# Loading x by image and channel at the start of a fused convolution chain, and its rows later

## The chip, the cores and the metric

The kernel runs on one core of a Trainium2 chip. A core has TensorE (PE in the profile), VectorE (DVE), ScalarE (ACT) and GpSimd (POOL), each with an instruction queue of its own, and SyncE (SP), which here only issues transfers. Sixteen DMA engines move all data between device memory and the on-chip buffer; SP, ACT and POOL can each put transfers on them. The metric is device microseconds (us) of one execution; less is better.

## The reference

The input x has 8 images, 16 channels and 64 x 64 pixels. Four blocks follow each other, each of the form `x = x + f(norm(x))`:

```
x = x + _L0_conv_ref(_gn(x), L0_conv_W, L0_conv_b)
x = x + _L1_conv_ref(_gn(x), L1_conv_weight)
x = x + _L2_conv_ref(_gn(x), ...)
x = x + _L3_conv_ref(_gn(x), L3_conv_combinator, L3_conv_bias)
```

`_gn` takes mean and variance of each image over groups of two channels and all pixels. The first block is a lattice of 4 x 4 cells; each cell is a 3 x 3 convolution with bias and ReLU that reads one to three results of other cells (16 channels each) and gives up to three. Only the last result, added to x, leaves the lattice. The other three blocks are single convolutions (one circular, one over spline features of the pixels, one plain).

## The kernel before, in words

**Layouts.** In the lattice a pixel row y of the image is cut as y = 4 q + r: the four rows r lie in different partitions, and even and odd pixel columns (s) in different halves, so a tile of one image has 2 x 4 x 16 = 128 partitions (s, r, channel) and 16 x 32 = 512 pixels. `X` holds all 8 images in this layout. Inputs and outputs of the cells lie in device memory (`lattice`, called `LAT` in the code), 32 rows of 2180 numbers for an image, where a row stands for a channel and a parity of the pixel row and is padded with zeros.

**Start, in the order of the text.** Each engine has its own stream of instructions; semaphores order them. SP and POOL load x into `XROW` by 32 transfers of 16 x 16 x 64 numbers, that is runs of one pixel row of 64 numbers, 256 bytes (L720, L812). ACT issues the small loads (identity `IDF`, raw weights `RAW`, biases, constants `CB` and `G`); TensorE waits for all six constants (`const_loaded`) before its first instruction. DVE clears buffers (`WX`, `KS`, the gaps, pieces of the weights, and the staging buffer `ST`, 128 x 6543 numbers). TensorE turns the weights of cell 0 (L1624), ACT and DVE split them into a high and a low part (L1077, L1274), POOL stores them as taps in device memory (`store_taps`, L845), clears the buffer (L838) and loads them spread over the partitions into `WA` (`spread_cell`, L853). DVE and ACT copy x from `XROW` to `X` (L1289, L1134), DVE takes statistics of each image (L1298, L1302), TensorE averages over the partitions of a group (L1693), DVE and POOL make scale and shift (POOL: L820, L822). ACT normalises one image at a time into one of three slots of `KS` (L1081), and POOL stores each by 4 transfers into `lattice` (L948), 32 in all.

**The lattice.** The 16 cells run one after the other, 8 images each: 128 steps (k, b), cell and image. For each step SP loads the input from `lattice` into one of four raw slots (L761), ACT rounds it to the high part (`split_hi`, L1098), DVE makes the low part and copies (`split_lo`, L1398 to L1410), TensorE multiplies (L1662), ACT adds the bias and applies ReLU into `ST` (`evacuate`, L1109), SP stores the result (L744), four steps behind the loads. ACT and DVE split two pieces ahead of TensorE. POOL spreads the weights of the next cell while one runs and waits at the end of each step for its evacuation. At cell 15 DVE adds the result to `X`; the later blocks work from there.

Of the kernel before, what the change touches and what calls it, by code (L numbers as in the profile page):

```python
# [6 lines left out]
P = 128  # L7
C = 16
WD = 64
# [10 lines left out]
YB = 8  # L20
BASES = 8
# [129 lines left out]
def build(nc, x, l0w, l0b, l1w, l2base, l2spline, l2scale, l2bias, l3w, l3bias, consts, out):  # L151
# [58 lines left out]
    RAW_STEPS.update({(8, 6): 12, (9, 4): 13, (10, 0): 14, (10, 6): 15})  # L210
    TURNS = ["cell0", "cell1"] + [TURN_STEPS[step] for step in sorted(TURN_STEPS)]
# [18 lines left out]
    with ctx:  # L230
# [47 lines left out]
        XROW = flat[:, 0:HALF * RQ * WD].rearrange("p (i y w) -> p i y w", i=HALF, w=WD)  # L278
        XS = KS[:, 0:3 * TOP].rearrange("p (z f) -> p z f", z=3)
# [57 lines left out]
        x_loaded = [sem(f"x_loaded{i}") for i in range(HALF)]  # L337
        x_loaded_pool = [sem(f"x_loaded_pool{i}") for i in range(HALF)]
        x_split, x_split_act = sem("x_split"), sem("x_split_act")
        const_loaded = sem("const_loaded")  # L340
# [9 lines left out]
        st_clear = sem("st_clear")  # L350
# [9 lines left out]
        input_stored = [sem(f"input_stored{b}") for b in range(B)]  # L360
        image_loaded = [sem(f"image_loaded{q}") for q in range(SLOTS_K)]
        tp_stored = sem("tp_stored")
        w_loaded = [sem("w_loaded0"), sem("w_loaded1")]
        w1_loaded, w2_loaded, w3_loaded = sem("w1_loaded"), sem("w2_loaded"), sem("w3_loaded")
# [6 lines left out]
        xn_ready = sem("xn_ready")  # L371
# [56 lines left out]

        def staged(s):

            return ST[:, s % SLOTS_S]

        def target_row(p, b, o, r):

            m = 1 if p is None else cells[p].m
            return first_row[p] + b * m * HALO + (r * m + o if m < 3 else 2 * o + r) * C
# [41 lines left out]
        def output_stores(s):  # L478
# [11 lines left out]
            else:  # L490
                yield from image_store(k, b, st)

# [169 lines left out]
        for par in range(2):  # L662
            n = 0
            for cell in cells[par::2]:
                n += dma_total(cell_spread(cell))
                w_after[cell.k] = n
# [48 lines left out]
        def _(sp):  # L715
            xv = x.rearrange("b c (q r) w -> b r c q w", r=4)
# [13 lines left out]
            load_taps(2)  # L730

# [14 lines left out]
            for s in range(STEPS):  # L746
# [9 lines left out]
                if k == 0:  # L756
                    sp.wait_ge(input_stored[b], 4 * 16)
                else:
                    sp.wait_ge(image_stored[b], 16 * stores_before[k])
# [46 lines left out]
        def _(pool):  # L806

            xv = x.rearrange("b c (q r) w -> b r c q w", r=4)
            for b in range(B):
                for y in range(2, 4):  # L810
                    rows = b % 2 * 4 * C + y * C
                    pool.dma_start(XROW[rows:rows + C, b // 2], xv[b, y]).then_inc(x_loaded_pool[b // 2], 16)  # L812
# [131 lines left out]
            norm(slice(0, B), slice(0, B), 1)  # L944
            for b in range(B):
                pool.wait_ge(xn_ready, b + 1)
                for dst, src in image_store(None, b, XS[:, b % 3]):
                    pool.dma_start(dst, src).then_inc(input_stored[b], 16)  # L948
            for s in range(STEPS):
# [6 lines left out]
                if k == 5 and b == 0:  # L956
                    for image in range(B):
                        pool.wait_ge(input_stored[image], 4 * 16)
# [14 lines left out]
                if k in (1, 2) and b in (1, 3):  # L973
                    half = 2 * (k - 1) + b // 2
                    pool.memset(flat[4 * C:P, half * PIECE:(half + 1) * PIECE], 0.0).then_inc(kr_clear, 1)
                if k + 1 < NC and k != 12:
# [85 lines left out]
        def _(act):  # L1062
            act.dma_start(IDF[:, :], consts[0:NG * C, P:P + NG * C]).then_inc(const_loaded, 16)
            for k in range(2):
                act.dma_start(RAW[k][:, :], l0w[0, k].rearrange("o i k d -> o (i k d)")).then_inc(raw_loaded[k], 16)
            act.dma_start(BN_IN[:, :], l0b.rearrange("a r (g c) -> (a r g) c", c=C)).then_inc(const_loaded, 16)
            act.dma_start(CB[:, :], consts[:, P + NG * C:P + NG * C + CB_COLUMNS]).then_inc(const_loaded, 16)
            act.dma_start(G[:, :], consts[:, 0:P]).then_inc(const_loaded, 16)
            act.dma_start(OB_IN[0:1, :], l2bias.rearrange("(a c) -> a c", a=1)).then_inc(const_loaded, 16)
            act.dma_start(OB_IN[1:2, :], l3bias.rearrange("(a c) -> a c", a=1)).then_inc(const_loaded, 16)  # L1070
# [59 lines left out]
            for i in range(HALF):  # L1130
                act.wait_ge(x_loaded[i], 4 * 16)
                act.wait_ge(x_loaded_pool[i], 4 * 16)
                for s in range(2):
                    last = act.activation(X[s * 4 * C:(s + 1) * 4 * C, 2 * i + 1].rearrange("p (y w) -> p y w", w=RX),  # L1134
                                          XROW[4 * C:P, i].rearrange("p y (w s) -> p s y w", s=2)[:, s], ACT.Copy)
                last.then_inc(x_split_act, 1)
            turned_hi_part("cell1")
            act.wait_ge(st_clear, 1)
            for b in range(B):
                act.wait_ge(norm_ready, 1)  # L1140
                if b >= 3:
                    act.wait_ge(input_stored[b - 3], 4 * 16)
# [706 lines left out]
```

## Time and profile before

| | |
|---|---|
| median of 3 runs | 1314.58 us (1313.54 to 1317.95) |
| the profiled execution | 1317.47 us, of which its span is 1315.7 us |
| busy share of the span | PE 89%, PEld 66%, DVE 59%, ACT 51%, POOL 30% |
| first and last convolution matmul of the lattice | 59.68 us and 1050.7 us into the span |
| moved by DMA | 232.12 MB, mean 176 GB/s |

The span is what the profile shows of the execution; the rest lies around it. PE is TensorE's matmuls, PEld its loading of weights, which runs beside them. A queue's name with a small q (SPq, POOLq) means the issuing of transfers.

### The profile page before, as it was taken

What the parts mean: (1) busy time and instruction counts of PE and PEld (TensorE: products, weight loads), DVE (VectorE), ACT (ScalarE), POOL (GpSimd) and SP (SyncE); (2) the same over time, 40 slices, a digit from 0 to 9 for tenths busy, and PEclk for the clock granted to TensorE, in tenths of its full rate; (3) what the DMA queues carried; (4) which work ended last, traced back from release to release, by engine and by line L of the source; (5) the groups of instructions that cost most, each with busy time, mean ns of one, the idle gap of its engine ahead of it and who ended that gap; (6) DMA issues with size and microseconds to landing.
All of it is one profiled execution on the core that took longest, in us unless ns stands there. A gap on an engine that the chain in (4) does not pass through costs nothing.

```text
span 1315.7 us, 14861 instructions
## 1 busy us (share of the span) xinstructions
PE 1175.0 (89%) x5088; PEld 870.3 (66%) x5088; DVE 775.1 (59%) x962; ACT 671.9 (51%) x724; POOL 391.3 (30%) x570
## 2 busy tenths in 40 slices
PE   1278898979999999999999999999999856999995
PEld 1155566756666667776666677777777745777773
DVE  5478895246656452225565653225665679899962
ACT  2357774335454444443545444334434588789921
POOL 5724243234450102122114032632123432103212
PEclk9999999989999999999999999999999977999997
DMA  9489998899999977889999996977789314577783
GB/s 88 122 205 232 243 279 228 221 189 188 221 194 218 192 195 193 220 194 171 217 196 206 213 225 175 254 210 211 193 190 204 53 31 70 84 115 120 114 125 57
DMA packets 108751, 232.12 MB, mean 176 GB/s; under 512 B 41332, under 2 KB 55236, under 8 KB 100484
## 3 DMA queue, kind: packets, MB, share of 16 engines
q1 hardware_dynamic: 91552, 205.02, 70.0%
q0 software_dynamic: 16576, 25.89, 10.7%
q8 instruction: 40, 0.66, 0.2%
q10 hardware_dynamic: 548, 0.27, 0.2%
q14 instruction: 35, 0.29, 0.1%
HBM read 122.05 MB, written 85.75 MB: 158 GB/s over the span
## 4 chain that ended last, share of the span: by engine, by line
PE 54%; SPq 15%; DVE 12%; issue 6%; DMA 6%; ACT 4%; POOL 3%; ACTq 0%; DVEq 0%; POOLq 0%
PE PB L1662 46%; SPq L761 11%; PE PB L1633 6%; SPq L744 3%; DMA S<-lattice 2%; DVE S L1500 2%; DVE F L1398 2%; ACT F L1098 2%; DVE S L1494 2%; DVE F L1410 2%; DVE F L1487 1%; DVE S L1507 1%; DMA F<-F 1%; PE PB L1624 1%; DMA lattice<-S 1%
## 5 line engine op out<-in xcount | busy, mean ns | idle before, releaser
L1662 PE MATMUL PB<-F,WA 128*96 128x512 f32 (+1 forms) x3792 | 922.0, 404 | 54.8 <-DVE F L1410 31.2
L1662 PEld LDWEIGHTS PB<-F,WA 128*96 128x96 f32 (+1 forms) x3792 | 663.6, 176 | 303.9 <-issue 56.0
L1098 ACT ACTIVATE F<-S 128x2116 fp32r<-128x2116 f32 (+4 forms) x160 | 261.7, 1637 | 271.5 <-DMA lattice<-S 122.3
L1109 ACT ACTIVATE S<-PB,BIAS 96x512 f32<-96x512 f32 (+1 forms) x320 | 209.5, 681 | 235.2 <-PE PB L1662 234.9
L1398 DVE TENSOR_TENSOR F<-S,F 128x1089 fp32r<-128x1089 f32 (+2 forms) x80 | 121.4, 1518 | 197.6 <-ACT F L1098 197.1
L1410 DVE CAST F<-F 64x528 fp32r<-64x528 f32 (+4 forms) x304 | 190.3, 675 | 3.5
L1400 DVE TENSOR_TENSOR F<-S,F 128x1058 fp32r<-128x1058 f32 x64 | 80.7, 1261 | 185.7 <-ACT F L1098 185.0
L1633 PE MATMUL PB<-F,WA 128*128 128x512 f32 x576 | 148.5, 416 | 20.6 <-DVE F L1487 20.6
L853 POOL DMA_DIRECT2D WA<-taps x84 | 61.0, 729 | 350.7 <-ACT S L1109 335.8
L1633 PEld LDWEIGHTS PB<-F,WA 128*128 128x128 f32 x576 | 113.2, 198 | 50.2 <-issue 21.8
L1401 DVE TENSOR_TENSOR F<-S,F 64x1058 fp32r<-64x1058 f32 x64 | 82.0, 1281 | 0.0
L845 POOL DMA_DIRECT2D taps<-WX x112 | 69.5, 685 | 22.6 <-ACT S L1109 13.5
L820 POOL TENSOR_TENSOR RS<-VE,NHALF 128x1 f32<-128x1 f32 (+1 forms) x25 | 25.1, 1003 | 129.4 <-DVE VE L1323 129.3
L838 POOL MEMSET WX<- 48x1600 f32 x18 | 26.1, 1452 | 116.6 <-ACT S L1109 94.7
L1404 DVE TENSOR_TENSOR F<-S,F 128x1089 fp32r<-128x1089 f32 x16 | 20.7, 1296 | 43.7 <-ACT F L1098 43.7
L1208 ACT ACTIVATE F<-S 128x2112 fp32r<-128x2112 f32 x16 | 31.5, 1968 | 26.8 <-DVE S L1507 14.5
L1081 ACT ACTIVATE KAN<-X,NBI,RS 64x512 f32<-64x512 f32 (+1 forms) x48 | 32.6, 679 | 20.1 <-POOL NBI L822 11.1
L1184 ACT ACTIVATE S<-KS,CB 128x528 f32<-128x528 f32 x64 | 41.9, 726 | 0.3
L1633 PE MATMUL PB<-F,WX 128*128 128x512 f32 x96 | 29.9, 471 | 13.5 <-DMA F<-F 13.5
L1487 DVE SCALAR_TENSOR_TENSOR F<-S,F 128x1056 fp32r<-128x1056 f32 x32 | 39.0, 1260 | 3.1 <-ACT F L1208 3.1
L1042 POOL DMA_DIRECT2D out<-OT x26 | 14.7, 579 | 84.8 <-DVE OT L1475 84.8
L1494 DVE SCALAR_TENSOR_TENSOR S<-S 128x2112 f32<-128x2112 f32 x16 | 37.7, 2354 | 2.4 <-ACT S L1192 2.4
(122 smaller groups left out, 720.3 us busy)
## 6 DMA issues: line engine op xcount, KB each, us to landing
lattice<-S SPq DMA_DIRECT2D x48, 817.5 KB, 6.3
S<-lattice SPq DMA_DIRECT2D x448, 66.1 KB, 5.1
lattice<-S SPq DMA_DIRECT2D x96, 272.5 KB, 4.0
S<-lattice SPq DMA_DIRECT2D x160, 136.1 KB, 3.0
S<-lattice SPq DMA_DIRECT2D x72, 272.5 KB, 5.5
S<-lattice SPq DMA_DIRECT2D x160, 70.1 KB, 2.9
S<-lattice SPq DMA_DIRECT2D x80, 136.2 KB, 4.9
S<-lattice SPq DMA_DIRECT2D x160, 66.0 KB, 2.9
```

The source lines that it names most:

```text
L761: sp.dma_start(dst, src).then_inc(image_loaded[q], 16)
L845: pool.dma_start(dst, src).then_inc(tp_stored, 16)
L853: pool.dma_start(dst, src).then_inc(w_loaded[k % 2], 16)
L1098: act.activation(piece_view(s, h, 0), raw_view(s, h), ACT.Copy).then_inc(hi_ready, 1)
L1109: act.activation(wide(to[:, at:at + TS])[:, :, 0:RX], pixels(RING_BANK[n % SLOTS_O][0:cell.rows, :]), ACT.Relu, bias=BIAS[0:cell.rows, k:k ...
L1398: last = nc.vector.tensor_tensor(lo, raw, hi, ALU.subtract)
L1400: nc.vector.tensor_tensor(lo[:, 0:2], raw[:, 0:2], hi[:, 0:2], ALU.subtract)
L1401: last = nc.vector.tensor_tensor(lo[0:4 * C, 2:4], raw[0:4 * C, 2:4], hi[0:4 * C, 2:4], ALU.subtract)
L1410: last = nc.vector.tensor_copy(FP[4 * C:P, slot, part, to:to + n], FP[0:4 * C, slot, 0, source:source + n])
L1494: nc.vector.scalar_tensor_tensor(A2[n % 2], AA[n % 2], 2.0, A2[n % 2], ALU.subtract, ALU.mult)\
L1633: last = nc.tensor.matmul(pixels(bank[:, :]), weights, moving, start=open_ and n == 0, stop=close and n == len(todo) - 1)
L1662: last = nc.tensor.matmul(bank, WA[0:rows, first:first + cell.rows], wide(FZ[0:rows, i % SLOTS_F, base:base + TS])[:, :, 0:RX], start=j == ...
```

## The change

x is loaded in its own order: 128 partitions are (image, channel), 4096 pixels each, in four transfers of 128 x 1024 numbers on SP into the memory of `X`, seen as `XC`. DVE takes statistics of 8 pieces of 512 pixels as they arrive and joins them into one mean and variance for each partition; TensorE averages over a pair of channels with a matrix `PAIR_MEAN`, made from `G`. Scale and shift are now one number for each partition. ACT and DVE normalise half of x each, in four instructions of 128 x 512 (`XN_ORDER`), into `XN`, which has the layout of `lattice` with all images below each other; SP stores images 0 and 1 by two transfers of 32 rows (`input_stores(0)`), POOL images 2 to 7 by two transfers of 96 rows.

Around it: SP, not POOL, loads cell 0's weights into `WA`; POOL, not DVE, clears `ST`; the weight and bias work that cell 0's start does not need follows the normalisation on DVE; TensorE's first instruction waits for `IDF` and `RAW` alone. The rows of x in the lattice's layout, which cell 15 adds, are loaded in the lattice: `X_LOADS` names eight steps of cells 7, 8, 11, 12, 13 and 14 in which POOL loads one image through `OT` by four transfers of 16 x 16 x 64, and two steps later (`X_SPLITS`) DVE and ACT copy half of it each into `X`. The edge values of the spline block are made by DVE at step (8, 3).

```diff
+    X_LOADS = {(7, 2): 0, (8, 1): 1, (8, 5): 2, (11, 3): 3, (12, 3): 4, (13, 1): 5, (13, 5): 6, (14, 2): 7}
+    X_SPLITS = {(k, b + 2): image for (k, b), image in X_LOADS.items()}
...
+        def input_stores(i):
+            rows = slice(0, FIRST * C) if i == 0 else slice(FIRST * C, P)
+            for r in range(2):
+                yield LAT[r * P + rows.start:r * P + rows.stop], XN[rows, r * PIECE:(r + 1) * PIECE]
...
-            for b in range(B):
-                for y in range(2):
-                    rows = b % 2 * 4 * C + y * C
-                    sp.dma_start(XROW[rows:rows + C, b // 2], xv[b, y]).then_inc(x_loaded[b // 2], 16)
+            xc, n = x.rearrange("b c h w -> (b c) (h w)"), HT * WD // XPARTS
+            for i in range(XPARTS):
+                sp.dma_start(XC[:, i * n:(i + 1) * n], xc[:, i * n:(i + 1) * n]).then_inc(channel_loaded[i], 16)
...
+            sp.wait_ge(tp_stored, tp_after["cell0"])
+            for dst, src in cell_spread(cells[0]):
+                sp.dma_start(dst, src).then_inc(w0_loaded, 16)
+            sp.wait_ge(xn_act, 1)
+            sp.wait_ge(xn_dve, 1)
+            for dst, src in input_stores(0):
+                sp.dma_start(dst, src).then_inc(input_stored[0], 16)
...
+            pool.memset(ST[:, :, :], 0.0).then_inc(st_clear, 1)
+            def load_x(b):
+                xv = x.rearrange("b c (q r) w -> b r c q w", r=4)
+                if b >= 2:
+                    pool.wait_ge(x_split, b - 1)
+                    pool.wait_ge(x_split_act, b - 1)
+                for y in range(4):
+                    pool.dma_start(OT[y * C:(y + 1) * C, b % 2], xv[b, y]).then_inc(x_loaded[b % 2], 16)
...
+            norm(slice(1, 2), slice(0, 1), 1)
             clear_taps("cell1")
-            spread_cell(0, 0, 1)
+            pool.wait_ge(xn_act, 1)
+            pool.wait_ge(xn_dve, 1)
+            for dst, src in input_stores(1):
+                pool.dma_start(dst, src).then_inc(input_stored[1], 16)
             store_taps("cell1")
...
             turned_hi_part("cell0")
+            act.wait_ge(norm_ready, 1)
+            act.wait_ge(xn_clear, 1)
+            for r, s, h in XN_ORDER[0::2]:
+                last = normalise(xn_rows(r, s, h), channel_rows(r, s, h), 0)
+            last.then_inc(xn_act, 1)
             turned_hi_part("cell1")
...
+                if (k, b) in X_SPLITS:
+                    image = X_SPLITS[k, b]
+                    dve.wait_ge(x_loaded[image % 2], 4 * 16 * (image // 2 + 1))
+                    nc.vector.tensor_copy(pixels(X[0:4 * C, image]), row_halves(image, 0)).then_inc(x_split, 1)
...
-            pe.wait_ge(const_loaded, 6 * 16)
-            pe.wait_ge(wa_clear, 1)
+            pe.wait_ge(idf_loaded, 16)
```

SP's stream from its first transfer to the first image loaded from `lattice`, before; a row is a line, what it writes and reads, its shape, and the semaphores it waits for:

```order
L720 DMA S<-in_x 16x16x64 x16
L727 DMA RAW_ONE<-in_L_conv_weight 16x144
L728 DMA RAW_ONE<-in_L_conv_combinator 16x144
L724 DMA RAW<-in_L_conv_W 48x432 [waits turned]
L761 DMA S<-lattice 32x1089 [waits input_stored0]
L761 DMA S<-lattice 32x561
L761 DMA S<-lattice 32x528
```

The same stretch of SP's stream after:

```order
L747 DMA X<-in_x 128x1024 x4
L754 DMA RAW_ONE<-in_L_conv_weight 16x144
L755 DMA RAW_ONE<-in_L_conv_combinator 16x144
L751 DMA RAW<-in_L_conv_W 48x432 [waits turned]
L760 DMA WA<-taps 64x4x64 [waits tp_stored]
L760 DMA WA<-taps 64x4x64
L760 DMA WA<-taps 64x2x64 x2
L760 DMA WA<-taps 64x4x64 x2
L760 DMA WA<-taps 64x2x64 x2
L764 DMA lattice<-S 32x2180 [waits xn_dve,xn_act]
L764 DMA lattice<-S 32x2180
L795 DMA S<-lattice 32x1089 [waits input_stored0]
```

Sixteen short loads are gone, and the eight weight loads and two long stores stand ahead of the first image.

POOL's stream from its first transfer to the scale of the normalisation (`RS`), before:

```order
L812 DMA S<-in_x 16x16x64 x16
L813 MEMSET TWOS 128x1
L814 MEMSET NHALF 128x8
L845 DMA taps<-WX 16x4x128 x8
L838 MEMSET WX 48x1600
L853 DMA WA<-taps 64x4x64 x2
L853 DMA WA<-taps 64x2x64 x2
L853 DMA WA<-taps 64x4x64 x2
L853 DMA WA<-taps 64x2x64 x2
L845 DMA taps<-WX 144x1x32 x8
L820 ISA
L820 TENSOR_TENSOR RS<-VE,NHALF 128x8
```

The same stretch of POOL's stream after, to the second taps:

```order
L842 MEMSET TWOS 128x1
L843 MEMSET NHALF 128x8
L844 MEMSET S 128x6543
L884 DMA taps<-WX 16x4x128 x8
L859 ISA
L859 TENSOR_TENSOR RS<-VE,NHALF 128x1
L861 TENSOR_TENSOR NBI<-GM,RS 128x1
L877 MEMSET WX 48x1600
L985 DMA lattice<-S 96x2180 x2
L884 DMA taps<-WX 144x1x32 x8
```

The 16 loads of x and cell 0's weight loads are gone, the clearing of `ST` (here `S`) has come, and the taps of cell 1 now stand behind the two stores.

POOL's stream in cell 7 after, around the load of image 0 (step (7, 2)); before, the same rows stood there without the two of L854:

```order
L892 DMA WA<-taps 64x1x288 [waits evac_done,out_done,tp_stored]
L854 DMA OT<-in_x 16x16x64 [waits evac_done]
L854 DMA OT<-in_x 16x16x64 x3
L892 DMA WA<-taps 64x1x288 x2
L877 MEMSET WX 48x1600 [waits tp_stored,evac_done]
L892 DMA WA<-taps 64x1x288
```

Four loads of x now stand ahead of later weight loads of the next cell.

## Rows read from the trace of the kernel before

**Rows 1.** The chain of work that ended last, first 60 us: start, length, what.

```profile
4.92 8.79 DMA OB_IN<-in_L_conv_bias
...
21.51 7.21 DMA taps<-WX
...
39.35 1.73 POOL RS L820
...
42.56 9.37 POOL lattice L948 x19
...
55.73 1.11 ACT F L1098
...
59.68 5.47 PE PB L1662 x12
```

**Rows 2.** Busy time, clock and DMA share by stretch (us from start: length, engines).

```profile
0.00:59.70 59.70, 4.57 (x43) 3.94 (x43) 27.85 (x85) 16.75 (x22) 41.80 (x81) 1.00 0.76 113
...
495.00:541.00 46.00, 46.00 (x205) 36.58 (x204) 10.96 (x9) 19.29 (x25) 9.72 (x13) 1.00 0.77 204
...
858.00:894.00 36.00, 36.00 (x165) 28.52 (x164) 9.81 (x9) 14.09 (x17) 8.43 (x11) 1.00 0.74 203
```

**Rows 3.** Timeline of the start: start, length, engine, line, what [idle before].

```profile
0.74 13.93 SPq L720 DMA_DIRECT2D S<-in_x  x16
1.13 1.39 DVE L1261 MEMSET WX<- 48x1600 f32 x1 [1.13 <-PEq L1836]
...
7.45 5.51 DVE L1269 MEMSET S<- 128x6543 f32 x1 [1.43 <-issue]
...
13.75 1.15 PE L1624 MATMUL PB<-IDF,RAW 48*16 48x32 f32 x18 [13.75 <-DMA OB_IN<-in_L_conv_bias]
...
14.98 1.28 ACT L1077 ACT_TABLE_LOAD   x1 [14.98 <-PE PB L1624]
...
16.71 0.44 DVE L1274 TENSOR_TENSOR WX<-PB,WX 16x288 fp32r<-16x288 f32 x1 [1.67 <-ACT WX L1077]
...
17.79 4.23 POOL L845 DMA_DIRECT2D taps<-WX  x8 [7.28 <-DVE WX L1274]
...
31.30 4.82 DVE L1298 BATCH_NORM_STATS2 STATS<-X 128x6 f32<-128x512 f32 x8
...
36.15 0.64 DVE L1302 BATCH_NORM_AGGREGATE MV<-STATS 128x2 f32<-128x6 f32 x8
...
41.45 2.23 ACT L1081 ACTIVATE KS<-X,NBI,RS 128x512 f32<-128x512 f32 x3 [10.71 <-POOL NBI L822]
...
46.08 13.44 SPq L761 DMA_DIRECT2D S<-lattice  x15
```

**Rows 4.** Transfers from issue to landing: RAW on ACT's queue (L1065), first 60 us.

```profile
DMA to landing us min/median/max: 4.0/4.6/5.2
```

**Rows 5.** The same for x in runs of 256 bytes on SP's queue (L720).

```profile
DMA to landing us min/median/max: 3.7/12.3/16.2
```

**Rows 6.** The same for taps stored by POOL from 30 to 60 us (L845).

```profile
DMA to landing us min/median/max: 1.8/1.9/1.9
```

**Rows 7.** The same for images loaded from the lattice, 40 to 100 us (L761).

```profile
DMA to landing us min/median/max: 2.4/3.5/4.8
```

**Rows 8.** The page's DMA issues: count, KB each, us to landing.

```profile
lattice<-S SPq DMA_DIRECT2D x48, 817.5 KB, 6.3
...
lattice<-S SPq DMA_DIRECT2D x96, 272.5 KB, 4.0
```

**Rows 9.** DMA rate in 40 slices of the first 60 us.

```profile
GB/s 0 102 145 114 104 119 94 95 89 94 90 93 100 96 100 111 132 145 0 0 3 112 66 87 37 35 26 0 0 138 141 197 237 283 242 270 263 247 127 223
```

**Rows 10.** Timeline in cell 1: POOL's clearing of raw slots, and DVE's copies.

```profile
102.49 1.91 POOL L975 MEMSET S<- 64x2180 f32 x1 [21.45 <-ACT S L1109]
102.53 4.28 DVE L1410 CAST F<-F 64x2180 fp32r<-64x2180 f32 x3
...
121.53 2.56 DVE L1410 CAST F<-F 64x2180 fp32r<-64x2180 f32 x3
```

More of the change, by code:

```diff
@@ L359, in build @@
         image_stored = [sem(f"image_stored{b}") for b in range(B)]
[L360 removed]
+        input_stored = [sem(f"input_stored{i}") for i in range(2)]
         image_loaded = [sem(f"image_loaded{q}") for q in range(SLOTS_K)]
@@ L663, in build @@
             n = 0
-            for cell in cells[par::2]:
+            for cell in cells[2 - par::2]:
                 n += dma_total(cell_spread(cell))
@@ L1129, in _ @@
             turned_hi_part("cell0")
[L1130 to L1136, printed above, removed]
-            turned_hi_part("cell1")
[L1138 to L1142, printed above, removed]
-                normalise(wide(XS[:, b % 3, 1:1 + TS])[:, :, 0:RX], pixels(X[:, b]), b).then_inc(xn_ready, 1)
-            act.wait_ge(bias_ready, 1)
+            act.wait_ge(norm_ready, 1)
[3 more added lines that the diff above has]
+            last.then_inc(xn_act, 1)
+            turned_hi_part("cell1")
             for i in range(2):
                 split_hi(piece_step(i), i - pieces_before[piece_step(i)])
+            act.wait_ge(st_clear, 1)
+            act.wait_ge(bias_ready, 1)
             for s in range(STEPS):
@@ L1162, in _ @@
                     turned_hi_part(TURN_STEPS[k, b])
+                if (k, b) in X_SPLITS:
+                    image = X_SPLITS[k, b]
+                    act.wait_ge(x_loaded[image % 2], 4 * 16 * (image // 2 + 1))
+                    act.wait_ge(xn_dve, 1)
+                    act.activation(pixels(X[4 * C:P, image]), row_halves(image, 1), ACT.Copy).then_inc(x_split_act, 1)
                 if k == NC - 1 and b >= 2:
@@ L1360, in _ @@
             nc.vector.tensor_copy(OB[:, :], BIAS_BANK[:, 64:66]).then_inc(bias_ready, 1)
-            u, w, f, cube = (EDGE[:, i, :] for i in range(4))
-            nc.vector.scalar_tensor_tensor(f, CB[:, 0:BASES], -1.0, CB[:, 0:BASES], ALU.mult, ALU.max)\
-                .then_inc(dve_step, 1)
-            dve.wait_ge(dve_step, next(steps))
-            nc.vector.tensor_scalar(u, f, 2.0, 2.0, ALU.min, ALU.subtract)
-            nc.vector.tensor_scalar(w, f, 1.0, 1.0, ALU.min, ALU.subtract).then_inc(dve_step, 1)
@@ L1377, in _ @@
-            dve.wait_ge(dve_step, next(steps))
-            nc.vector.tensor_copy(EDGE_HI[:, :], f).then_inc(dve_step, 1)
-            dve.wait_ge(dve_step, next(steps))
-            nc.vector.tensor_tensor(cube, f, EDGE_HI[:, :].bitcast(F32), ALU.subtract).then_inc(dve_step, 1)
-            dve.wait_ge(dve_step, next(steps))
-            for part, value in enumerate((EDGE_HI[:, :].bitcast(F32), cube)):
-                for odd in range(2):
-                    rows = slice(odd * 4 * C, (odd + 1) * 4 * C)
-                    last = nc.vector.tensor_copy(EDGE_ROW[rows, :, part],
-                                                 value[rows].rearrange("p (t o) -> p t o", o=2)[:, :, odd])
@@ L1684, in _ @@
             turn("cell0")
+            pe.wait_ge(mv_ready, 1)
+            nc.tensor.matmul(STAT_BANK[1][:, 2:4], PAIR_MEAN, MV[:, 1, :],
+                             start=True, stop=True).then_inc(group_ready, 1)
+            turn("cell1")
             pe.wait_ge(bias_rep, 1)
@@ L1690, in _ @@
                              start=True, stop=True).then_inc(bias_done, 1)
-            turn("cell1")
-            pe.wait_ge(mv_ready, 1)
-            nc.tensor.matmul(STAT_BANK[1][:, 0:2 * B], G[:, :], MV[:, :, :].rearrange("p b a -> p (b a)"),
-                             start=True, stop=True).then_inc(group_ready, 1)
+            pe.wait_ge(wa_clear, 1)
             for s in range(STEPS):
```

176 lines of the change are left out of this document (102 added, 74 removed).

## The prediction

> **What bounds the kernel now.** I read the chain of waits first, because the change works on the start. The first convolution matmul of the lattice begins at 59.68 us, and in the chain ahead of it no stretch is TensorE's work of any size: a late constant (8.79 us), the landing of cell 0's taps (7.21), then scale and shift, and from 42.56 us POOL's 32 short stores of the normalised images one behind the other [rows 1]. The reader should see there that the start is a line of transfers and small instructions. The stretch table says the same: in 59.70 us TensorE is busy for 4.57, while the DMA share is 0.76 at only 113 GB/s, which is the mark of short runs [rows 2]. Later it is the other way round: in the stretches of cells 7 and 12 TensorE is busy for 46 of 46 and 36 of 36 us, DVE for 10 to 11 and ACT for 14 to 19, with a DMA share of 0.77 and 0.74 [rows 2]. So a microsecond off the start should come through as one, if the lattice behind it runs as before, and work put on DVE, ACT, POOL or the DMA in those cells lies beside TensorE.
>
> **The start after the change, step by step.** Two lines meet at SP's store of images 0 and 1. All times are counted from the span's start.
>
> *Weights.* `RAW` and `IDF` are now first on ACT's queue, issued by about 1.2 us, as the engines begin at 1.1 [rows 3]; `RAW` took 4.0 to 5.2 us to land while x was loading [rows 4], so 5.2 to 6.4, and I take 5.2. Turning is 1.15, the table load 1.28, ACT's half about 0.4, DVE's 0.44 [rows 3]: about 8.6, hand-overs included. DVE is free by then, since its long clearing is now 4360 numbers (3.7 us at the rate of 6543 in 5.51 [rows 3]) behind one of 1.39 and a small one: 6.4 us. POOL clears `ST` from about 1.5, after two small ones; its own clearing of 2180 numbers took 1.91 us [rows 10], so 6543 take 5.7 and end at 7.2. POOL then issues the eight taps stores, 4.23 us after a hand-over of half a microsecond [rows 3]: done at 13.4, landed at 15.6 with a little over the 1.9 us that such stores take when the x load is out of the way [rows 6]. SP issues the eight weight loads behind that; POOL needs 0.53 for one, SP needed 0.87 for one of x with a full queue [rows 3], and I take 0.6: SP is free at **20.4**.
>
> *x.* 2.10 MB in runs of 4 KB. The trace has no such load. Its short runs went at 94 to 145 GB/s, the long rows of the lattice at up to 283 [rows 9]. 4 KB is nearer to the 8.7 KB rows than to 256 bytes, so I take 230: 9.1 us, and with 1.9 for a landing the last part is there at 11.7. The statistics of the last two pieces take 1.2 (8 in 4.82 [rows 3]): 12.9. From the end of the statistics (36.12) to the scale on POOL (39.35) it was 3.2 us with eight joinings; with one it is 2.7 [rows 1, 3], so 15.6. POOL has finished its taps stores by then. From the scale's start to ACT's first normalisation it was 2.1 us (39.35 to 41.45 [rows 1, 3]): 17.7. Four instructions on ACT at 0.74 [rows 3] end at **20.7**; DVE does its four in the same time. So both lines arrive together, and the later is 20.7.
>
> *Store, load, split.* SP's second store is issued at 21.3. Alone, 272.5 KB took 4.0 us, 817.5 KB took 6.3 [rows 8]; POOL's two stores of 837 KB run beside it, so I take 6.3: 27.6. Three loads of image 0 at 0.6, the last landing 3.5 us after its issue [rows 7]: 32.3. From ACT's first split to the first matmul it was 3.95 us (55.73 to 59.68 [rows 1]): **36.3**. That is 23.4 us earlier than 59.68.
>
> *Images 2 to 7* come from POOL's stores, issued from 20.7 on. All stores together are 2.23 MB, 8 to 9 us at 240 to 283 GB/s [rows 9], landed at about 31.5. SP reaches image 2 at 31.2, so it hardly waits; the image is split by about 40.2, and TensorE, which needed 5.47 us for its first image [rows 1], is not done with two before that. Behind POOL's wait for the normalisation stand only the taps of cell 1, which are wanted when cell 0 has ended, some 30 us later.
>
> *Moved off the start.* The clearing of weights, the bias work and cell 1's turning follow DVE's normalisation and lie under the 15 us in which SP stores and loads. The edge values are 16 tiny DVE instructions in cell 8, a cell like cell 7, where DVE is idle for three quarters of the time [rows 2]: nothing.
>
> *x in rows, in the lattice.* Per image POOL issues four loads (2.1 us at 0.53), DVE and ACT each copy 64 x 512. At the start eight such images took about 27 us with the engines nearly full (issue until 14.67, then 12.3 to land [rows 3, 5]), 3.4 us of all DMA engines for an image; three images in cells 7 and 8, some 92 us together, lift the share from 0.77 to about 0.88 [rows 2]. What could hurt is a late landing, because DVE and ACT wait for it in their streams, and the splits and evacuations of the lattice queue behind them. POOL issues after step b - 1; DVE waits after the split for step b + 4, about two steps later, ACT another step later, and TensorE then still has two split images. A step is an eighth of a cell, 5.75 us in cell 7 and 4.5 in cell 12 [rows 2]. TensorE is therefore reached after about 4 steps, 18 to 23 us. Issue and landing are 5.8 to 18.3 us (3.7 to 16.2 [rows 5]). I take zero; at the far end cell 12's image just touches TensorE.
>
> **Sum.** The profiled execution took 1317.47 us; minus 23.4 is 1294.1. It lies 2.9 above the median of 1314.58, so by the median I forecast **1291**.
>
> **Where a row and a rule part.** While POOL cleared 2180 numbers, three DVE copies took 4.28 us in place of 2.56 [rows 10]: the two engines shut each other out. If POOL's clearing of `ST` and DVE's of `XN` do the same, the later one ends 3.7 us later, the weights reach SP at 24.1, and the first matmul moves from 36.3 to 39.7: 1294.5. The nearest row, a DVE clearing beside POOL's issuing, ran at the same rate as ever, so I take no such wait. The Trainium skill, "SBUF — State Buffer", section "Who interferes with whom", lists copies, casts and tensor_scalar among the VectorE instructions that can exclude GpSimd, and not a memset on this chip; by it the sum stays 1291, by the row of the copies it would be 1294.5. The trace has no pair of clearings to decide.
>
> **Rivals.**
> - *The two clearings take turns*: 1294 to 1296, as above. For it speaks the row of the copies, against it that a clearing reads nothing. Chance 0.16.
> - *Long runs come no faster than short ones.* x at 114 GB/s lands at 21, the first matmul is at 45.6, and if the stores run at that rate too, images 2 and up are another 6 late: 1300 to 1306. For it: the mean of the start. Against it: the rows of the lattice. Chance 0.12.
> - *Slower or no change: the row loads stop TensorE.* Each of the eight images would have to stop it by 2.9 us to give back 23.4, so its load would take 21 to 26 us from POOL's issue, against 5.8 to 18.3 here. In that case 1310 and more, and slower from 3.5 us an image. For it: DMA shares of 0.74 to 0.77 in these cells and runs of 256 bytes. Chance 0.05.
> - *The change does less than it says because the lattice's first cells are bound by SP and not by TensorE's start.* Then the shift is that of SP's first load, from 46.1 [rows 3] to 27.6, or 18.5 us: 1296. Against it: SP's fifth image waits for the split of the first (`raw_read`), so SP is there before TensorE. Chance 0.09.
>
> **Numbers.** The forecast's own case, 1286 to 1294, has 0.58. Its early end: stores at 4.0, landing at 2.4, x not binding gives a first matmul at 32.6, 27.1 us earlier, 1287.5, and 2 for the spread of runs. The range is **1285 to 1301**: it takes in the turns of the clearings, SP's bound and the near end of slow x. A measurement of this kernel can tell about 0.3%, 4 us. Faster by more than that needs 1310.6 or less, which only the third rival misses: faster 0.95, same 0.03, slower 0.02.
>
> **What would show it.** In the changed profile: the last statistics at about 13 us, the scale on POOL at about 16, ACT's normalisation at 18 to 21, SP's first lattice load at about 28, the first convolution matmul at 36; TensorE's stretches of cells 5 to 14 as long as before; DVE's and ACT's waits for `x_loaded` short. The forecast is wrong if SP waits long for taps or for `XN`, if the clearings overlap with one stretched, or if TensorE shows new gaps at cells 7, 8 and 11 to 14.

## The result and the profile after

| | before | after |
|---|---|---|
| median of 4 runs side by side | 1316.26 us (1313.54 to 1318.79) | 1302.69 us (1301.75 to 1307.1) |
| the profiled execution, of which span | 1317.47, 1315.7 us | 1307.1, 1304.2 us |
| first lattice matmul | 59.68 us | 38.10 us |

The ratio (after to before) is 0.9903, 95% interval 0.9875 to 0.9931: faster, by 13.6 us or 1.0%, where 23.4 us were forecast. Two more series of the changed kernel (below) gave 1301.01 and 1299.74; over all its 14 runs the median is 1301.5, against 1315.5 over 48 runs of the kernel before: 14.0 us. 1302.69 lies 1.7 us outside the range on record.

The page's busy times after, beside the shares in the table of before:

```profile
PE 1179.5 (90%) x5088; PEld 874.7 (67%) x5088; DVE 772.4 (59%) x959; ACT 671.2 (51%) x720; POOL 382.3 (29%) x549
```

**The start.** The two clearings, in the timelines of POOL and of DVE (start, length, engine, line, what):

```profile
0.80 5.55 POOL L844 MEMSET S<- 128x6543 f32 x1
...
3.52 3.69 DVE L1300 MEMSET S<- 128x4360 f32 x1 [0.86 <-issue]
```

They lie over each other for 2.8 us and neither is stretched: by POOL's 1.91 us for 2180 numbers [rows 10] its 6543 take 5.73, by DVE's 5.51 for 6543 [rows 3] its 4360 take 3.67. So the rival of the two clearings is refuted, though DVE's copies were slower beside a clearing by POOL [rows 10]. The Trainium skill's list of what can exclude GpSimd ("SBUF — State Buffer", "Who interferes with whom") names no memset on this chip, and this trace agrees.

The chain of waits from the end of the normalisation to the first lattice matmul (start, length, what); it answers to [rows 1]:

```profile
21.05 0.32 SPq L764
21.36 0.04 issue
21.41 4.36 DMA lattice<-S
25.77 0.02 issue
25.78 0.30 SPq L795
26.09 0.04 issue
26.13 1.97 SPq L795
28.09 0.04 issue
28.14 5.97 DMA S<-lattice
34.11 0.02 issue
34.13 1.12 ACT F L1136
...
38.10 5.35 PE PB L1711 x12
```

SP's stores go out at 21.05 (forecast 20.7) and land at 25.77 (27.6). The loads of image 0 stand at 25.78 instead of 27.6 and still land later, at 34.11 instead of 32.3: their second issue takes SP 1.97 us, and the third takes 5.97 us from the start of its issue to its landing, where lattice loads took 3.5 [rows 7]. POOL's stores of images 2 to 7 are in flight beside them.

**The lattice.** The lead over the kernel before is the difference of the times at which TensorE comes to the same place. A turn is the 18 small matmuls by which TensorE turns a later cell's weights, at a fixed step (cell, image):

| place | before | after | lead |
|---|---|---|---|
| first lattice matmul | 59.68 | 38.10 | 21.6 |
| turn in (1, 2) | 111.77 | 91.06 | 20.7 |
| turn in (8, 2) | 559.43 | 541.40 | 18.0 |
| turn in (9, 0) | 604.66 | 590.54 | 14.1 |
| turn in (12, 2) | 873.26 | 858.54 | 14.7 |
| span | 1315.7 | 1304.2 | 11.5 |

The steadiest of these losses is the one between (8, 2) and (9, 0): 45.23 us before, 49.14, 49.20 and 51.92 in the three profiles of the changed kernel. Between (1, 2) and (8, 2) this profile loses 2.7 us, most of it by a wait of 2.32 us in cell 5, at 297.4 us. The other two lose 2.1 and 2.2 us there, at other places, and over all 13 profiles of the changed kernel and of its variants in the experiments it is anything from 2.9 us lost to 2.8 gained, 0.4 lost on average: the spread of executions more than the change. Behind (12, 2) it is alike: from there to the end the kernel before takes 442.4 us, the changed one 445.6, 442.0 and 439.9. TensorE around cell 9's start, before and then after:

```profile
591.25 13.48 PE L1662 MATMUL PB<-F,WA 128*96 128x512 f32 x56 [1.14 <-DVE F L1410]
```

```profile
575.63 14.99 PE L1711 MATMUL PB<-F,WA 128*96 128x512 f32 x56 [3.54 <-DVE F L1449]
```

It stands idle for 3.54 us instead of 1.14, and the same 56 matmuls then take 14.99 us instead of 13.48. The stretch tables, of before and then of after, have it (length, busy times of PE, PEld, DVE, ACT and POOL, granted clock, DMA share, GB/s):

```profile
591.00:604.70 13.70, 13.46 (x57) 9.06 (x58) 7.03 (x9) 5.53 (x6) 2.01 (x2) 1.00 0.94 179
```

```profile
575.00:590.60 15.60, 14.97 (x57) 10.09 (x58) 10.16 (x15) 6.90 (x8) 2.02 (x2) 0.89 0.92 176
```

The granted clock is 0.89, a mean of the levels of 2.4 and 1.2 GHz, right behind the idle time; before, with 1.14 us idle, it was 1.00, the upper level. Idle time and clock together are 3.9 us. What TensorE waits for is image 0 of cell 9, and SP loads it. SP and POOL at that place, before:

```profile
569.12 12.62 SPq L761 DMA_DIRECT2D S<-lattice  x16
```

```profile
570.17 5.31 POOL L845 DMA_DIRECT2D taps<-WX  x8 [0.77 <-issue]
```

And after:

```profile
551.09 14.41 SPq L795 DMA_DIRECT2D S<-lattice  x16
```

```profile
551.37 5.31 POOL L884 DMA_DIRECT2D taps<-WX  x8
556.21 1.05 POOL L854 DMA_DIRECT2D OT<-in_x  x1
```

The eight tap stores (cell 10's taps, in runs of 128 bytes) start 1.05 us after SP's first load before, with an idle 0.77 us of POOL ahead of them, and 0.28 us after it now, without. SP's sixteen issues take 1.8 us longer. One line's answer over these sixteen (duration of an issue in ns, least, median, most; then the landing), after:

```profile
L795 SPq DMA_DIRECT2D S<-lattice x16: 420/592/2151, 551.1 to 564.9; - x16
...
DMA to landing us min/median/max: 4.2/4.7/6.2
```

The median issue is the same as before (601 ns); a few are stretched, one to 2.15 us (before, the longest was 1257 ns).

The row loads themselves do what the prediction said of them. All 32 transfers, from issue to landing, and neither DVE nor ACT waits for them:

```profile
L854 POOL DMA_DIRECT2D OT<-in_x x32: 562/572/1047, 490.2 to 950.8; - x32
...
DMA to landing us min/median/max: 2.6/4.2/7.0
```

### The profile page after: what moved, and what is told of

It is laid out like the page before. It is cut to its first block, busy times and chain, and to the rows that moved or that the text cites. A ratio compares the mean times of both kernels' runs of the same rounds, so it can differ in the third digit from the quotient of the medians.

```text
span 1304.2 us, 14844 instructions
## 1 busy us (share of the span) xinstructions
PE 1179.5 (90%) x5088; PEld 874.7 (67%) x5088; DVE 772.4 (59%) x959; ACT 671.2 (51%) x720; POOL 382.3 (29%) x549
## 3 DMA queue, kind: packets, MB, share of 16 engines
q0 software_dynamic: 16032, 25.98, 10.5%
## 4 chain that ended last, share of the span: by engine, by line
PE 54%; SPq 16%; DVE 12%; DMA 6%; issue 5%; ACT 5%; POOL 1%; ACTq 0%; DVEq 0%; POOLq 0%
PE PB L1711 46%; SPq L795 13%; PE PB L1680 6%; DMA S<-lattice 2%; SPq L778 2%; ACT F L1136 2%; DMA lattice<-S 2%; DVE S L1548 2%; DVE S L1542 2%; DVE F L1535 1%; DVE S L1555 1%; DVE F L1437 1%; DMA F<-F 1%; DVE F L1449 1%; SPq L826 1%
## 5 line engine op out<-in xcount | busy, mean ns | idle before, releaser
L1449 DVE CAST F<-F 64x528 fp32r<-64x528 f32 (+4 forms) x304 | 186.7, 663 | 3.5
L1680 PE MATMUL PB<-F,WA 128*128 128x512 f32 x576 | 149.5, 419 | 20.3 <-DVE F L1535 20.1
L892 POOL DMA_DIRECT2D WA<-taps x76 | 56.6, 746 | 340.0 <-ACT S L1147 321.7
L884 POOL DMA_DIRECT2D taps<-WX x112 | 67.9, 655 | 18.1 <-ACT S L1147 13.2
L859 POOL TENSOR_TENSOR RS<-VE,NHALF 128x1 f32<-128x1 f32 x25 | 24.4, 975 | 134.7 <-DVE VE L1335 134.6
L1244 ACT ACTIVATE F<-S 128x2112 fp32r<-128x2112 f32 x16 | 31.5, 1967 | 27.8 <-DVE S L1555 14.9
L1443 DVE TENSOR_TENSOR F<-S,F 128x1089 fp32r<-128x1089 f32 x16 | 20.7, 1296 | 40.3 <-ACT F L1136 40.2
L1680 PE MATMUL PB<-F,WX 128*128 128x512 f32 x96 | 31.5, 490 | 13.6 <-DMA F<-F 13.6
L1080 POOL DMA_DIRECT2D out<-OT x26 | 14.7, 571 | 85.5 <-DVE OT L1523 85.5
## 6 DMA issues: line engine op xcount, KB each, us to landing
lattice<-S SPq DMA_DIRECT2D x48, 817.5 KB, 6.0
```

The lines of the kernel that those rows point to most:

```text
L884: pool.dma_start(dst, src).then_inc(tp_stored, 16)
L892: pool.dma_start(dst, src).then_inc(w_loaded[k % 2], 16)
L1449: last = nc.vector.tensor_copy(FP[4 * C:P, slot, part, to:to + n], FP[0:4 * C, slot, 0, source:source + n])
L1680: last = nc.tensor.matmul(pixels(bank[:, :]), weights, moving, start=open_ and n == 0, stop=close and n == len(todo) - 1)
```

## The experiments

All are made from the changed kernel. The letters of theories are those of the expectations. The C of the first three (a lattice that starts earlier is slower in itself) is not the C of the held taps and behind (the place of POOL's burst). Medians of one kernel differ by 1 to 3 us between series, so differences of 3 us are read from the profiles, at their place, and the medians say only whether they are in line.

**The changed kernel again, loads earlier, no row loads** (one series, before at 1315.65).

> The changed kernel itself, once more, for a second profile of it. In the first one TensorE began its first convolution matmul 21.6 us earlier than before, but this lead had shrunk to 18.0 us by the second half of cell 5, to 14.1 us by cell 9 and to about 11.5 us at the end. Theory A (the loads of x rows collide with the lattice's own loads): the loss of 3.9 us between cell 8 and cell 9 is there again, and that of 3.3 us in cell 5, where no x row is loaded, is not. Rival B (the losses are the chance of one execution): neither comes back in its place, and the time goes up and down by them. Rival C (a lattice that starts earlier is slower in itself): both are there again.

> The three loads of x rows of cells 7 and 8 are moved earlier, so that none is in the air when SP begins the long loads of cell 9: steps (7, 1), (7, 5) and (8, 1) in place of (7, 2), (8, 1) and (8, 5). Theory A: the 3.5 us gap of TensorE at the start of cell 9 goes, cell 9 starts about 18 us ahead of the kernel before, and the time falls by some 3 to 4 us, to about 1299. Rivals B and C: no change of the time beyond 1 us.

```diff
-    X_LOADS = {(7, 2): 0, (8, 1): 1, (8, 5): 2, (11, 3): 3, (12, 3): 4, (13, 1): 5, (13, 5): 6, (14, 2): 7}
+    X_LOADS = {(7, 1): 0, (7, 5): 1, (8, 1): 2, (11, 3): 3, (12, 3): 4, (13, 1): 5, (13, 5): 6, (14, 2): 7}
```

> The x rows are not loaded at all: no transfers of x in the lattice, no copies, and the last cell adds what the memory of X holds (it leaves out the input that is added to the lattice's result, so its output differs). All else is the changed kernel. It gives what the row loads cost in all. Theory A: 4 to 8 us less than the changed kernel, 1295 to 1299, with the lead of the start kept to the end of cell 14 but for 1 or 2 us. Rival C: within 1 us of the changed kernel. My forecast's price for the row loads was zero, which is C's number.

```diff
-    X_LOADS = {(7, 2): 0, (8, 1): 1, (8, 5): 2, (11, 3): 3, (12, 3): 4, (13, 1): 5, (13, 5): 6, (14, 2): 7}
+    X_LOADS = {}
...
-                    dve.wait_ge(x_split, b + 1)
-                    dve.wait_ge(x_split_act, b + 1)
```

Measured: again 1301.01 (ratio 0.9894, 0.987 to 0.9918); earlier 1299.04 (0.9876, 0.9854 to 0.9898); without rows 1297.57 (0.9862, 0.9841 to 0.9883). In the second profile the loss between (8, 2) and (9, 0) is there again, with an idle time of 3.59 us, and the wait at 297 us is not, as theory A has it. The earlier loads came out at the 1299 us that A names, but not by the gap that it names. With the loads earlier no x load is in flight when SP loads cell 9, and TensorE still waits there for 3.04 us, with 14.41 us for SP's sixteen issues. So the collision of an x load with SP's loads is not the cause. Without row loads the idle time is 0.72 us and the issues take 12.35, and the median is 3.4 us under the changed kernel's, near A's 4 to 8 and not the 1 us of C: the loss does hang on the row loads, but not through their transfers at that moment.

**Rows late, the taps held, and both** (one series, before at 1314.44).

> The changed kernel with the first five row loads moved out of cells 7, 8 and 11 into cells 11 and 12 (images 0 to 4 at (11,0), (11,3), (12,0), (12,3), (12,5)); the other three stay. Theory A (the row loads, their copies, or the place that POOL's own issues take because of them, hold back cell 9's loads): with none of them ahead of cell 9, TensorE's idle time at the start of cell 9 falls from 3.5 to about 1 us, its first 56 matmuls there take 13.5 instead of 15 us, and the lead of some 22 us is kept past (9,0); median about 1297.5, some 3.5 below the changed kernel's 1301. Theory B (the loads cost wherever they stand, since the lattice's transfers are the tight resource): the loss comes back in cells 11 and 12, and the time stays at 1300 to 1301.

```diff
-    X_LOADS = {(7, 2): 0, (8, 1): 1, (8, 5): 2, (11, 3): 3, (12, 3): 4, (13, 1): 5, (13, 5): 6, (14, 2): 7}
+    X_LOADS = {(11, 0): 0, (11, 3): 1, (12, 0): 2, (12, 3): 3, (12, 5): 4, (13, 1): 5, (13, 5): 6, (14, 2): 7}
```

Measured: 1297.46 (0.9865, 0.984 to 0.989). At cell 9 SP's issues took 12.83 us, POOL's idle 0.77 us is back, and (8, 2) to (9, 0) took 45.61. But TensorE stood at another place:

```profile
877.55 7.69 PE L1711 MATMUL PB<-F,WA 128*128 128x512 f32 x25 [3.18 <-DVE F L1449]
```

There the load of image 4 comes directly behind cell 15's tap stores. The landing of SP's loads from 847.9 to 850.6 us, ahead of the tap stores, and then from 861.9 to 866.2 us, beside them and the load of image 4:

```profile
DMA to landing us min/median/max: 2.1/2.2/2.4
```

```profile
DMA to landing us min/median/max: 2.9/3.7/5.5
```

So this expectation's first theory held at cell 9, and a part of the second in cell 12: right behind a burst, a row load does cost. In the better place below, where no row load stands behind these tap stores, the same nine loads beside them landed in 2.7 to 3.2 us.

> The changed kernel, all row loads and copies where they are, but POOL's eight tap stores of cell 10 (runs of 128 bytes) are issued two steps later, in (8,6) and not in (8,4). Theory C (SP's sixteen load issues for (9,0) are stretched from 0.6 us to 1.3 to 1.9 us each while those eight stores go out, and the row loads only shift POOL's instructions so that they meet SP's issues some 0.8 us earlier): SP's sixteen issues then take about 10 us instead of 14.1 to 14.4, cell 9's first load lands some 3 us earlier, TensorE's idle time at its start falls from 3.5 to under 1 us, and the median is 1296.5 to 1298. Theory D (the row loads themselves, their transfers or the copies on DVE and ScalarE, are what is late): the gap stays at 3 to 3.6 us and the time at 1300 to 1301.

```diff
-                if b >= 2 and (k, b - 2) in TURN_STEPS and TURN_STEPS[k, b - 2] not in ("circular", "conv"):
-                    store_taps(TURN_STEPS[k, b - 2])
+                lag = 4 if k == 8 else 2
+                if b >= lag and (k, b - lag) in TURN_STEPS and TURN_STEPS[k, b - lag] not in ("circular", "conv"):
+                    store_taps(TURN_STEPS[k, b - lag])
```

Measured: 1298.80 (0.9878, 0.9852 to 0.9904). SP and TensorE:

```profile
546.67 10.47 SPq L795 DMA_DIRECT2D S<-lattice  x16
```

```profile
568.43 13.48 PE L1712 MATMUL PB<-F,WA 128*96 128x512 f32 x56 [0.78 <-DVE F L1450]
581.84 1.30 PE L1672 MATMUL PB<-IDF,RAW 48*32 48x32 f32 x18
586.50 42.03 PE L1712 MATMUL PB<-F,WA 128*96 128x512 f32 x168 [3.36 <-DVE F L1450]
```

With all row loads and copies in place, the sixteen issues fell to 10.47 us and the idle time at the cell's start to 0.78. The burst of tap stores makes SP slow. It now met the next image's loads, five of which took a median of 1755 ns to issue, and TensorE waited 3.36 us there: the loss was moved by one image, so the time did not fall by the 3 to 4 us.

> The changed kernel, but POOL issues cell 1's eight tap stores only when image 0 has been loaded from the lattice; its two long stores of images 2 to 15 stay where they are. If the tap stores are what stretches SP's loads of image 0 (issues of 1.97, 2.52 and 1.58 us where others take 0.42, the last one landing 5.97 us after its issue), the four issues take about 1.7 us, the last lands near 31 and the first lattice matmul comes at 34.5 to 35.5 us instead of 38.1, 3 us of the median. If the long stores' 1.67 MB do it, issues and landings stay and the first matmul stays at 38.

```diff
+            pool.wait_ge(image_loaded[0], loads_after[0])
             store_taps("cell1")
```

Measured: 1299.60 (0.9882, 0.9856 to 0.9907). First matmul at 37.94 us, loads of image 0 landing in 5.1 to 5.9: at the start it is not the taps. (POOL's long stores hold images 2 to 7; the "2 to 15" of two expectations is a slip.)

> The three together: late row loads, cell 10's tap stores two steps later, cell 1's tap stores after image 0. If each is worth what theories A, C and the tap stores at the start give it (A and C are two ways to the same 3.5 us, not a sum), first lattice matmul at 35, no gap over 1 us at cell 9, and a median of about 1294; if none, 1301.

It is the last three edits together. Measured: 1299.32 (0.9883, 0.9857 to 0.9909). First matmul at 37.58; both moved waits came back, 2.52 us at 583.0 and 1.99 at 876.4. The gains did not add up, as two of the edits had only carried their wait elsewhere and the third had gained nothing.

**Only the phase, a better place, and quiet stores** (one series, before at 1316.14).

> The changed kernel once more, beside the three below. 1301 to 1302.5 by its two earlier medians; TensorE's idle time at the start of cell 9 again 3.5 to 3.6 us, with SP's sixteen issues for (9,0) taking over 14 us, if these belong to the kernel and not to one execution.

Measured: 1299.74 (0.9891, 0.9863 to 0.992), idle time 5.15 us, issues 14.23: the wait belongs to the kernel.

> The changed kernel with one tiny POOL operation (a power of one column, 0.56 us in the start) put ahead of cell 10's eight tap stores in (8,4), and nothing else changed. In the kernel before and without row loads POOL has an idle 0.78 us at that place and its first tap store comes 1.06 us after SP's first issue for (9,0); in the changed kernel it has none, and comes 0.28 us after. Theory C (only the phase of POOL's burst against SP's issues counts): with the burst some 0.6 us later, SP's sixteen issues take 12.4 to 12.9 us, the idle time at cell 9 falls from 3.5 to between 0.7 and 1.5 us. Rival (phase is not it, what the burst does to SP depends on the row loads being about): the sixteen issues stay above 14 us and the gap at 3 to 3.6.

```diff
+        SCR = sb("SCR", [P, 1])
...
+                    if k == 8:
+                        pool.tensor_tensor(SCR[:, :], TWOS[:, 0:1], NHALF[:, 0:1], ALU.pow)
                     store_taps(TURN_STEPS[k, b - 2])
```

Measured: 1299.25 (0.9881, 0.9849 to 0.9913; 1295.02 to 1308.36), a median that shows nothing. The profile does. POOL, SP and TensorE:

```profile
547.64 0.59 POOL L1041 TENSOR_TENSOR SCR<-TWOS,NHALF 128x1 f32<-128x1 f32 x1
548.18 5.34 POOL L885 DMA_DIRECT2D taps<-WX  x8
```

```profile
547.33 13.11 SPq L796 DMA_DIRECT2D S<-lattice  x16
```

```profile
570.14 13.48 PE L1714 MATMUL PB<-F,WA 128*96 128x512 f32 x56 [1.82 <-DVE F L1452]
```

Half a microsecond of useless work on POOL, and nothing else, took (8, 2) to (9, 0) from 49.1 to 51.9 down to 45.88 us. Idle time and issues came out a little above the expected bounds (1.82 against 1.5, 13.11 against 12.9), with the burst 0.85 us behind SP's first load and not 1.06.

> Row loads late as in the earlier run, but none right behind a burst of tap stores: there the load of image 4 in (12,5) came directly behind cell 15's taps, SP's loads took up to 5.5 us to land instead of 2.3, and TensorE stood for 3.2 us at 877. Here images 0 to 4 at (11,0), (11,2), (11,3), (12,0), (12,2). Theory: no gap over 1.5 us at cells 9 and 12, the lead of 21 to 22 us kept to cell 14, median 1295 to 1297. Rival (the row loads' 2 us each come out wherever they stand): a gap of 2 to 3 us at another place in cells 11 or 12, median 1298 to 1300.

```diff
-    X_LOADS = {(7, 2): 0, (8, 1): 1, (8, 5): 2, (11, 3): 3, (12, 3): 4, (13, 1): 5, (13, 5): 6, (14, 2): 7}
+    X_LOADS = {(11, 0): 0, (11, 2): 1, (11, 3): 2, (12, 0): 3, (12, 2): 4, (13, 1): 5, (13, 5): 6, (14, 2): 7}
```

Measured: 1297.85 (0.9867, 0.9843 to 0.9891), no idle time over 1.5 us in cells 9 to 12, and (12, 2) reached 23.3 us ahead of the kernel before. The theory held at its places; the median is 0.9 over its bound and within 0.2 of the rival's.

> The changed kernel, but POOL issues its two long stores of images 2 to 15 (and so cell 1's tap stores behind them) only when image 0 has been loaded. If the long stores are what slows the loads of image 0 (landing 5 to 6 us instead of 2.3 to 2.5), they land at 30 instead of 34 and the first lattice matmul comes at 34, 4 us earlier; but images 2 and on then land some 8 us later, at about 42, and are wanted from 40 on, so that TensorE waits some 4 us in cell 0 and the time stays within 1 us of the changed kernel. If SP's issues are slow for another reason, the first matmul stays at 38 and the time is 4 us or more above.

```diff
+            pool.wait_ge(image_loaded[0], loads_after[0])
             for dst, src in input_stores(1):
```

Measured: 1298.58 (0.9872, 0.9846 to 0.9898). Image 0's loads (issue in ns, and landing), and TensorE:

```profile
L795 SPq DMA_DIRECT2D S<-lattice x3: 303/421/423, 25.6 to 26.4; - x3
...
DMA to landing us min/median/max: 2.3/2.3/2.3
```

```profile
32.87 7.49 PE L1712 MATMUL PB<-F,WA 128*128 128x512 f32 x24 [9.37 <-DVE F L1450]
44.14 5.46 PE L1712 MATMUL PB<-F,WA 128*128 128x512 f32 x12 [3.78 <-DVE F L1450]
```

The first matmul came 5.2 us earlier than in the changed kernel, and 3.8 were given back waiting for image 2. The tap stores, held here too, had made no difference by themselves, so POOL's long stores are what slows SP's loads at the start.

**Both mended** (before at 1316.25; "the last run but one" is the better place, "the last run" the quiet stores).

> Row loads placed as in the last run but one, and POOL's stores of the normalised input in two parts: images 2 and 3 at once (0.55 MB), images 4 to 7 only when image 0 has been loaded. Theory (what slows image 0's loads is the bytes of POOL's long stores in flight at the same time; with a third of them the loads land between the 2.3 us of the held stores and the 5 to 6 us of the changed kernel): first lattice matmul at 34 to 36 us, no wait for image 2 (it was 3.8 us with all stores held), turn in (1,2) at 87 to 88 instead of 90, and a median 1.5 to 3 us under the last run but one, 1295 to 1296.5. Rival (any store in flight beside them does it, or images 4 to 7 become late): first matmul at 37 to 38 or a new wait of 3 us in cell 0, and the time within 1 us of 1297.9.

```diff
-            rows = slice(0, FIRST * C) if i == 0 else slice(FIRST * C, P)
+            rows = slice((0, 2, 4)[i] * C, (2, 4, B)[i] * C)
...
-                    sp.wait_ge(input_stored[0 if b < FIRST else 1], 2 * 16)
+                    sp.wait_ge(input_stored[min(b // 2, 2)], 2 * 16)
...
-            for dst, src in input_stores(1):
-                pool.dma_start(dst, src).then_inc(input_stored[1], 16)
+            for i in (1, 2):
+                if i == 2:
+                    pool.wait_ge(image_loaded[0], loads_after[0])
+                for dst, src in input_stores(i):
+                    pool.dma_start(dst, src).then_inc(input_stored[i], 16)
```

Measured: **1292.34** (1287.65 to 1301.35; ratio 0.9828, 0.9793 to 0.9863), faster than the kernel before, and than the changed one, whose interval in its longest series begins where this one ends (0.9891, 0.9863 to 0.992). Image 0's loads and TensorE:

```profile
L795 SPq DMA_DIRECT2D S<-lattice x3: 303/964/1175, 25.6 to 27.2; - x3
...
DMA to landing us min/median/max: 3.1/3.4/3.4
```

```profile
34.31 10.31 PE L1714 MATMUL PB<-F,WA 128*128 128x512 f32 x36 [10.69 <-ACT F L1139]
```

The first matmul is at 34.31 with no wait for image 2, and the turn in (1, 2) is at 85.12. The median fell 5.5 us below the better place's, more than the 1.5 to 3 expected; the profile shows 4.0 at the first matmul, and the runs spread by 13.7 us, so the rest is not placed.

What all fourteen profiles say of cell 9, by where POOL's burst begins against SP's first load for (9, 0):

| burst begins | kernels | SP's sixteen issues | (8, 2) to (9, 0) |
|---|---|---|---|
| 0.28 us after | changed (three profiles), rows earlier, taps of cell 1 held, quiet stores | 14.04 to 14.41 us | 48.3 to 51.9 us |
| 0.85 to 1.06 us after | before, no rows, rows late, phase alone, better place, both mended | 12.35 to 13.12 us | 44.8 to 45.9 us |
| 10.5 and 11.9 us after | taps of cell 10 held, the three together | 10.47 and 10.49 us | 44.9 and 43.9 us, then a wait of 3.4 and 2.5 |

## Why the prediction was wrong, step by step

The direction and the mechanism of the start were right: the first lattice matmul moved by 21.6 us of the 23.4 forecast, and the chain there is the one described, with one exception below. The size was wrong, and two steps made it so.

**"I take zero" for x in rows in the lattice: the step that failed.** It asked whether x would land too late for DVE and ACT, and there it was right (2.6 to 7.0 us against a cover of 18 to 23). It also let the DMA share rise to 0.88; from (7, 2) to (8, 2) it went from 0.79 to 0.84. What it didn't ask is what else POOL issues, and when: with the row loads among POOL's instructions, an idle 0.77 us of POOL no longer stands ahead of the burst of tap stores in (8, 4), the burst starts 0.8 us earlier against SP's loads for cell 9, a few of those issues are stretched, and TensorE waits longer at a place where it already waited 1.14 us before. That cost 3.9 us of idle time and clock in the profile after, 3.9 to 6.7 in the three profiles from (8, 2) to (9, 0). The delay of POOL alone shows this cause; that the transfers of x or the copies do it is refuted by the loads moved earlier and by the held taps. The condition "if the lattice behind it runs as before" is what did not hold.

**Store and load at the start, a mis-sized term.** The store landed in 4.36 us, not 6.3, but the loads of image 0 then met POOL's 1.67 MB and landed in 6.0 to 6.7, not 3.5, with SP's issues at 1.97 and 2.52 instead of 0.6. Net 1.8 us late (38.10 for 36.3). Holding those stores gave landings of 2.3 and a first matmul at 32.87, near the forecast's early end of 32.6. The 4.0 and 6.3 us of [rows 8] are medians over the lattice, with other transfers about, and not of a store alone; the 837 KB beside them are the page's 817.5 KB in thousands of bytes.

**Statistics: an overlap that was not there.** The prediction lets the statistics run as x arrives, so that only the last two pieces follow its landing. In DVE's order they stand behind cell 0's turning (8.80) and an instruction that waits for `G` (from the chain of waits):

```profile
2.13 7.75 DMA G<-in_consts
...
10.20 4.76 DVE STATS L1361 x8
```

The last part of x was there at 9.7 us, its issue at 2.13 and 7.5 to land, not at 11.7; DVE began at 10.11, had all eight pieces to do, and ended at 14.95, not 12.9. The scale came at 17.06 for 15.6, and the first normalisation followed it by 0.9 us, not 2.1, so that the normalisation ended at 21.0 for 20.7. That this end fits is luck: steps that were 2.1 us too short, then 0.6 and 1.2 too long. SP was free from the weights at 20.7 for 20.4. A reading to set right: the short runs in [rows 9] went down to 89 GB/s, not 94.

**The rivals.** The clearings in turns are refuted by their timelines. Slow long runs are refuted too, as x landed at 9.7 us and not at 21; that 1302.69 lies in this rival's 1300 to 1306 is chance. A lattice bound by SP at its first cells would have moved only as far as SP's first load, 20.3 us (46.08 to 25.78); with the quiet stores and with both mended this load stands at 25.6 too, and the turn in (1, 2) came 23.9 and 26.7 us earlier. The row loads that stop TensorE are what happened, but through another engine's stream and at one cell only, so by 4 us and not by 23.

**What stays open.** 23.4 less 1.8 and 3.9 to 6.7 is 14.9 to 17.7, and the medians show 14.0. The two kernels without the wait at cell 9 and with the start as it was (no rows 18.1, better place 18.3 us by medians) also show some 3 us less than their first matmuls lead; the intervals of the ratios reach to 20.9 and 20.7 us. In their profiled executions the whole lead is there: the spans are 22.3 and 21.3 us under that of before, with first matmuls 21.7 and 21.4 us earlier. But these executions lie 2.4 and 1.7 us under their kernels' medians, and the one of before 2.0 above its own. So the 3 us lie in the spread of executions, and no profile shows a place for them.

What POOL's idle 0.77 us is was not tried. It has no releaser in the trace. Counted through POOL's transfers from the start, it stands ahead of the 183rd: in the changed kernel a row load of (8, 1), in the kernels with no or later row loads the first tap store of the burst (the 185th with both mended, which issues two more at the start). The changed kernel, and then the one without rows:

```profile
533.49 0.56 POOL L854 DMA_DIRECT2D OT<-in_x  x1 [0.77 <-issue]
```

```profile
547.01 5.28 POOL L884 DMA_DIRECT2D taps<-WX  x8 [0.78 <-issue]
```

In two kernels (rows earlier, the three together) the 183rd comes right behind a wait of 16.0 or 11.6 us, where such a pause cannot be seen. So by the traces the row loads, standing among these transfers, take the pause away from the burst; why POOL pauses there stays open.

## What to carry to other kernels

A transfer that is added to a queue moves everything that the queue issues behind it, so price not only its own landing but what the next burst on that queue will meet on the others. Look for the places where the critical engine already waits a little (here 1.14 us of waiting at cell 9 before, which grew from there), and ask of each neighbour's stream what half a microsecond either way does there. A store that nobody waits for yet can still be the cause of a late load: let the small, urgent transfers go first and split the long ones by when they are wanted.

## What was not expected of the hardware

The issuing of a transfer on SP is not of a fixed length: 0.3 to 0.42 us for image 0 with POOL's stores held, 0.6 us as the median in cell 9, up to 2.40 us while POOL's tap stores in runs of 128 bytes go out (cell 10's taps held), and up to 2.72 us at the start beside POOL's long stores (cell 1's taps held). The Trainium skill, "DMA: Bandwidth & Descriptors", section "Issuing engines are not separate DMA queues", says that transfers begun by different engines run on the same DMA engines and interleave; the trace agrees, with landings of 2.3 us alone and 6.0 to 6.7 beside POOL's stores, and shows besides that the issuing engine itself is held up.

Eight such tap stores cost SP by their place against its first load: 14.0 to 14.4 us for sixteen issues when they begin 0.28 us behind it, 12.4 to 13.1 at 0.85 to 1.06, and 10.5 without them. Why half a microsecond matters so much is not shown.
